# Two mixture-of-experts layers around a state-space block: the first layer's expert outputs stored in slot order and fetched by place

## What is computed

```python
x = L0_attn_x                                                  # (4, 512, 128)
x = _layernorm(x + _L0_attn_ref(x, L0_attn_W_qkv, L0_attn_W_out), axis=-1)
x = _layernorm(x + _L0_ffn_ref(x, ...), axis=-1)
x = _layernorm(x + _L1_attn_ref(x, ...), axis=-1)
x = _layernorm(x + _L1_ffn_ref(x, ...), axis=-1)
```

## Time and profile before

| what | us |
|---|---|
| median of 3 runs (lowest, highest) | 663.41 (660.64, 665.27) |
| the profiled execution's own time | 663.71 |
| its span, first to last instruction | 661.9 |
| first layer: routing and shared MLP | about 74 to 96 |
| first layer: slots | about 96 to 199 |
| fetches to the start of the state loop | about 199 to 235 |
| state loop, four sequences | about 235 to 476 |
| second mixture: routing, slots, end | about 476 to 662 |

### The profile page before, as it was taken

How to read it: one execution, slowest core, us unless ns; L and a number is a source line. 1 busy time by engine, 2 the same in 40 slices (tenths; PEclk the granted TensorE clock), 3 DMA queues, 4 the chain that set the end, 5 groups by cost and what they waited for, 6 DMA issues and landing times.

```text
span 661.9 us, 8700 instructions
## 1 busy us (share of the span) xinstructions
PE 554.6 (84%) x2858; PEld 370.4 (56%) x2858; DVE 419.7 (63%) x756; ACT 361.4 (55%) x640; POOL 383.4 (58%) x303
## 2 busy tenths in 40 slices
PE   6988889999997569679967986988788699999980
PEld 3666556777665224225323532433347699999950
DVE  2444581111106899999999999999967544444456
ACT  3544564555452657944795597768423255555423
POOL 1011117777771246995797689678821677677451
PEclk9999998999999879869988998898989699999986
DMA  4154101111117844343344334433200111111142
GB/s 111 47 179 149 44 7 50 48 47 52 47 39 246 332 172 155 131 158 128 132 139 165 128 127 144 162 123 132 81 16 1 40 42 48 43 43 45 28 130 63
DMA packets 35148, 65.78 MB, mean 99 GB/s; under 512 B 6112, under 2 KB 23208, under 8 KB 34465
## 3 DMA queue, kind: packets, MB, share of 16 engines
q1 hardware_dynamic: 29824, 51.19, 23.2%
q0 software_dynamic: 4992, 9.32, 5.5%
q10 hardware_dynamic: 288, 4.72, 2.0%
HBM read 57.60 MB, written 8.52 MB: 100 GB/s over the span
## 4 chain that ended last, share of the span: by engine, by line
PE 36%; DVE 34%; issue 10%; POOL 9%; ACT 6%; DMA 3%; SPq 0%; POOLq 0%; DVEq 0%; ACTq 0%
DVE wide L1631 11%; DVE ps L1624 6%; PE ps L646 5%; PE ps L650 5%; DVE w L1631 5%; PE ps L658 5%; PE ps L673 4%; PE ps L797 3%; PE ps L686 3%; ACT work L1168 2%; PE ps L679 2%; POOL rows L1807 2%; DVE work L1496 2%; POOL y_choice L1815 1%; DVE work L1407 1%
## 5 line engine op out<-in xcount | busy, mean ns | idle before, releaser
L1807 POOL DMA_INDIRECT rows<-xn_rows,source x78 | 76.2, 977 | 59.0 <-DVE dest L1422 22.1
L1631 DVE TENSOR_TENSOR_SCAN wide<-work,ps 128x1024 f32<-128x1024 f32 x43 | 98.2, 2284 | 1.3
L797 PE MATMUL ps<-wide,ident 128*128 128x512 f32 x128 | 72.1, 691 | 24.6 <-POOL wide L1779 24.6
L1624 DVE TENSOR_TENSOR ps<-ps,w 128x1024 f32<-128x1024 f32 x64 | 78.9, 1233 | 6.9 <-DVE wide L1631 0.5
L1446 DVE COPY xT<-ps 128x128 f32<-128x128 f32 x78 | 22.5, 288 | 83.1 <-PE ps L668 81.5
L797 PE MATMUL ps<-w,ident 128*128 128x512 f32 x124 | 63.5, 641 | 10.5 <-POOL w L1779 10.5
L1779 POOL TENSOR_TENSOR wide<-wide,w 128x1024 f32<-128x1024 f32 x22 | 51.9, 2358 | 32.4 <-DVE wide L1631 32.3
L1168 ACT ACTIVATE work<-work,a_neg 128x512 f32<-128x512 f32 x86 | 56.7, 711 | 19.7 <-DVE wide L1631 17.2
L1451 DVE TENSOR_TENSOR wide<-wide,ps 128x512 f32<-128x512 f32 x39 | 26.8, 688 | 62.5 <-PE ps L650 61.3
L797 PEld LDWEIGHTS ps<-wide,ident 128*128 128x128 f32 x128 | 24.9, 208 | 61.3 <-POOL wide L1779 38.2
L1779 POOL TENSOR_TENSOR w<-wide,w 128x1024 f32<-128x1024 f32 (+1 forms) x21 | 49.0, 2337 | 12.5 <-DVE wide L1631 12.4
(11 more groups left out here) (273 smaller groups left out, 1174.1 us busy)
## 6 DMA issues: line engine op xcount, KB each, us to landing
w<-bc_rows SPq DMA_DIRECT2D x64, 512.0 KB, 3.7
w<-in_w ACTq DMA_DIRECT2D x2, 2304.0 KB, 9.8
w<-y_choice SPq DMA_DIRECT2D x16, 256.0 KB, 3.8
wg<-in_wg SPq DMA_DIRECT2D x1, 2304.0 KB, 11.2
wu<-in_wu SPq DMA_DIRECT2D x1, 2304.0 KB, 16.1
wd<-in_wd SPq DMA_DIRECT2D x1, 2304.0 KB, 21.1
rows<-xn_rows,source POOLq DMA_INDIRECT x78, 2.6
work<-in_x SPq DMA_DIRECT2D x4, 256.0 KB, 2.8
```

What stands on the lines that cost most here:

```text
L797: last = mm_(bank(6 + h), ident[:, :], hc[j % 4][:, h, :], start=False, stop=(j == NS - 1))
L1624: V.tensor_tensor(dbu, du, bc_all[j % 4][:, 0:S].unsqueeze(1).to_broadcast([P, EH, S]), ALU.mult)\
L1631: V.tensor_tensor_scan(st[n % 3].rearrange("p h t -> p (h t)"), dA[n % 3].rearrange("p h t -> p (h t)"), dbu.rearrange("p h t -> p (h t)") ...
L1807: G.indirect_dma_start(out=xin[i % RING][:, :], out_offset=None, in_=xn_rows, in_offset=bass.IndirectOffsetOnAxis(ap=source[:, i:i + 1], a ...
```

## The change

In the first layer only:
- SP stores each slot's output as it stands to `y_slots`, one row per place in the sorted order. The scatters are gone; `dest` is not computed. `posf`, cast to an integer (`place`), says where each token's two rows lie. After the last store has landed GpSimd fetches them: 16 tiles times 2 choices, 32 indirect DMAs (`fetch`).
- VectorE copies each slot's 512 up columns to `own_g`, two slots ahead (`up_weights`). Four products with the copy as the stationary matrix replace the one of 512 columns, the four transposes of the hidden values and the copy to `hT`. The output product of slot i stands in step i, no longer one step later.
- ScalarE issues the loads of `wg`, `wu` and `wd` at steps 4, 13 and 22 of the slot loop.
- Groups 2 and 3 are combined and normalised inside the state loop's first sequence: `combine` and `variances` between product and scan of states 1 and 4, `norm_group` at states 3 and 6. Their choices lie in `nT_all` and their base in `x_all`. Group 0 is combined tile by tile as its fetches land.
- TensorE's last shared products wait for the third tile's fetches in place of SP's.

```diff
@@ -196,8 +197,16 @@
-        all_stats, all_mv = (wide[:, T + at:T + at + NT * n] for at, n in ((0, 6), (96, 2)))
-        all_stats = all_stats.rearrange("p (t s) -> p t s", s=6); all_mv = all_mv.rearrange("p (t s) -> p t s", s=2)
+        all_stats = sb("all_stats", [P, NT, 6]); all_mv = sb("all_mv", [P, NT, 2])
...
+        def base_tile(l, t):
...
+            return x_tile(t) if l == 0 and t >= 2 * QT else tile_of(base[l], t)
...
+        def y_tile(l, c, t):
...
+            return tile_of(nT_all, c * 2 * QT + t - 2 * QT) if l == 0 and t >= 2 * QT else tile_of(y_k[c], t)
@@ -319,6 +331,7 @@
+        LOAD_AT = {4: (wg, "wg"), 13: (wu, "wu"), 22: (wd, "wd")}
@@ -398,19 +411,23 @@
+                if l == 0:
+                    for i in range(ROUTED):
+                        sp.wait_ge(*yout_set[0].at(i + 1))
+                        sp.dma_start(y_slots[i * P:(i + 1) * P, :], yout[i % RING][:, :]).then_inc(slot_sent[i % RING], 16)
+                    return
...
-            load_weights(ld_f1, (wg, "wg"), (wu, "wu"), (wd, "wd"))
@@ -660,32 +677,28 @@
-                    x, h, t, y = i + 2, i + 1, i, i - 1
+                    x, h, y = i + 2, i + 1, i
...
-                        e = expert_of(h)
-                        pe.wait_ge(*xT_set[l].at(h + 1))
-                        last = mm_(bank(hbank[0] + p), xT[p][:, :], wa[:, ds(e, HID)], start=True, stop=True)
-                    if valid(t):
-                        p = i % 2
-                        pe.wait_ge(*hs_set[l].at(t + 1))
+                        pe.wait_ge(*xT_set[0].at(h + 1))
+                        pe.wait_ge(weights_in, h + 1)
...
-                            last = tr(ps[:, 2 + p, j * P:(j + 1) * P], hs[p][:, j * P:(j + 1) * P], ident[:, :])
-                        last.then_inc(hT_ps[l].sem, 1)
+                            last = mm_(ps[:, hbank[0] + p, j * P:(j + 1) * P], own_g[p][:, j * P:(j + 1) * P], xT[p][:, :],
+                                       start=True, stop=True)
...
-                        pe.wait_ge(*hT_set[l].at(y + 1))
+                        pe.wait_ge(*hs_set[0].at(y + 1))
...
-                            last = mm_(bank(y_bank[l][p], D), hT[p][:, j * P:(j + 1) * P], wc[:, ds(e + j * D, D)],
+                            last = mm_(bank(y_bank[0][p], D), hs[p][:, j * P:(j + 1) * P], wc[:, ds(e + j * D, D)],
@@ -701,10 +714,9 @@
-            pe.wait_ge(*hT_set[0].at(ROUTED))
...
-            pe.wait_ge(*gathered[0][0].at(32))
+            pe.wait_ge(first_fetched[2], 32)
@@ -1024,21 +1036,20 @@
-                    h, t, y = i + 1, i, i - 1
+                    h, y = i + 1, i
...
-                    if valid(t):
-                        p = i % 2
-                        act.wait_ge(*hT_ps[l].at(t + 1))
-                        cp(hT[p], bank(2 + p)).then_inc(hT_set[l].sem, 1)
...
-                        wait_pos(act, ys_sent[l][q], y // RING * 16)
-                        cp(yout[q][:, :], bank(y_bank[l][y % 2], D)).then_inc(yout_set[l].sem, 1)
+                        if y >= RING:
+                            act.wait_ge(slot_sent[q], y // RING * 16)
+                        cp(yout[q][:, :], bank(y_bank[0][y % 2], D)).then_inc(yout_set[0].sem, 1)
+                    if i in LOAD_AT:
+                        dst, name = LOAD_AT[i]
+                        act.dma_start(dst[:], a[name]).then_inc(ld_f1, 16)
@@ -1418,6 +1429,9 @@
+                    if l == 0:
+                        V.tensor_copy(place[:, :], posf[:, :, :].rearrange("p k t -> p (k t)")).then_inc(idx_set[0].sem, 1)
+                        return
@@ -1437,6 +1451,10 @@
+                def up_weights(i):
+                    e = expert_at(mybir.EngineType.DVE, 0, i)
+                    V.tensor_copy(own_g[i % 2], w1[:, ds(e, HID)]).then_inc(weights_in, 1)
@@ -1451,9 +1469,15 @@
+                    if l == 0 and valid(i + 3) and i >= -1:
+                        dve.wait_ge(*h_ps[0].at(i + 2))
+                        up_weights(i + 3)
...
+                    dve.wait_ge(*expert_set[0].at(1))
+                    up_weights(0)
+                    up_weights(1)
@@ -1482,18 +1506,31 @@
-                V.tensor_tensor(tiles(base[l][:, b * S:(b + 1) * S]), x_seq(b), tiles(bank(sy_bank(l, b))),
+                V.tensor_tensor(x_seq(b) if l == 0 and b >= 2 else tiles(base[l][:, b * S:(b + 1) * S]), x_seq(b), tiles(bank(sy_bank(l, b))),
...
-                own = [tile_of(base[l], b * QT + q) for q in range(QT)]
-                dve.wait_ge(*gathered[l][b % 2].at((b // 2 + 1) * 32))
+                own = [base_tile(l, b * QT + q) for q in range(QT)]
+                if l:
+                    dve.wait_ge(gathered[b % 2], (b // 2 + 1) * 32)
...
+                if l == 0 and b == 0:
+                    for q in range(QT):
+                        dve.wait_ge(first_fetched[q], 32)
+                        link(V.scalar_tensor_tensor(out=own[q], in0=tile_of(y_k[0], q), scalar=gates[0][:, q:q + 1],
+                                                    in1=own[q], op0=ALU.mult, op1=ALU.add))
+                        link(V.scalar_tensor_tensor(out=own[q], in0=tile_of(y_k[1], q), scalar=gates[1][:, q:q + 1],
+                                                    in1=own[q], op0=ALU.mult, op1=ALU.add))
+                        link(V.bn_stats(all_stats[:, q, :], own[q]))
+                        steps.mark(V.bn_aggr(all_mv[:, q, :], all_stats[:, q, :]))
+                    return
+                if l == 0:
+                    dve.wait_ge(y_fetched[b - 1], QT * 32)
...
-                        steps.mark(V.scalar_tensor_tensor(out=own[q], in0=tile_of(y_k[k], t), scalar=gates[k][:, t:t + 1],
+                        steps.mark(V.scalar_tensor_tensor(out=own[q], in0=y_tile(l, k, t), scalar=gates[k][:, t:t + 1],
@@ -1637,6 +1674,12 @@
+                        if b == 0 and j in (1, 4):
+                            g = 2 + j // 4
+                            combine(0, g)
+                            variances(0, g)
+                        if b == 0 and j in (3, 6):
+                            norm_group(1 + j // 3)
@@ -1658,14 +1701,8 @@
-            combine(0, 2)
-            variances(0, 2)
...
-            combine(0, 3)
-            variances(0, 3)
-            norm_group(2)
...
-            norm_group(3)
@@ -1780,6 +1817,8 @@
+                    if b == 0 and j in (1, 4):
+                        inverse_group(0, 2 + j // 4)
@@ -1787,8 +1826,23 @@
-                for g in range(NB):
-                    inverse_group(0, g)
...
+                def fetch(t):
+                    for c in range(2):
+                        G.indirect_dma_start(out=y_tile(0, c, t), out_offset=None, in_=y_slots,
+                                             in_offset=bass.IndirectOffsetOnAxis(ap=place[:, c * NT + t:c * NT + t + 1], axis=0))\
+                            .then_inc(first_fetched[t] if t < QT else y_fetched[t // QT - 1], 16)
...
+                pool.wait_ge(*idx_set[0].at(2))
+                for k in range(RING):
+                    pool.wait_ge(slot_sent[k], 16 * fetches(k))
+                for t in range(QT + 1):
+                    fetch(t)
+                inverse_group(0, 0)
+                for t in range(QT + 1, NT):
+                    fetch(t)
+                    if t == 2 * QT + 2:
+                        inverse_group(0, 1)
@@ -1807,7 +1861,7 @@
-                    if i >= RING:
+                    if l and i >= RING:
```

More of the change, by code:

```diff
@@ L100, in build @@
         y_choice = nc.dram_tensor("y_choice", (2 * T, D), F32).ap()
+        y_slots = nc.dram_tensor("y_slots", (ROUTED * P, D), F32).ap()
         bc_rows = nc.dram_tensor("bc_rows", (NB * NS, 2 * S), F32).ap()
@@ L163, in build @@
         held_i = sb("held_i", [P, ROUTED], U32); source = sb("source", [P, ROUTED], U32)
-        dest = sb("dest", [P, ROUTED], U32)
+        dest = sb("dest", [P, ROUTED], U32); place = sb("place", [P, PAIRS], U32)
         slot_e = sb("slot_e", [P, ROUTED], I32)
@@ L289, in build @@
         yout_set = layers("yout_set", ROUTED)
-        ys_sent_ = [layers(f"ys_sent{k}", 16 * fetches(k)) for k in range(RING)]
+        ys_sent_ = [layers(f"ys_sent{k}", 0) for k in range(RING)]
+        slot_sent = [sem(f"slot_sent{k}") for k in range(RING)]
         ys_sent = [[r[l] for r in ys_sent_] for l in range(2)]
-        gathered_ = [layers(f"gathered{k}", NB // 2 * 32) for k in range(2)]
-        gathered = [[r[l] for r in gathered_] for l in range(2)]
+        gathered = [sem(f"gathered{k}") for k in range(2)]
+        first_fetched = [sem(f"first_fetched{q}") for q in range(QT)]
+        y_fetched = [sem(f"y_fetched{b}") for b in range(1, NB)]
+        weights_in = sem("weights_in")
         fix_mid = sem("fix_mid")
@@ L1527, in norm_group @@
                 for t in range(g * QT, g * QT + QT):
-                    last = V.tensor_scalar(x_tile(t), tile_of(base[0], t), all_mv[:, t, 0:1], inv2[:, 0, t:t + 1],
```

(1 more changed line is left out.)

18 lines of the change are left out of this document (9 added, 9 removed).

## The result

The changed kernel takes 668.28 us (median of 8 runs, 666.52 to 671.17), the kernel before 663.88 us (8 runs, 660.64 to 665.27). The ratio is 1.0065, with a 95% interval from 1.0047 to 1.0083: 4.4 us slower, within the 1% that was named, and inside the range. The forecast was 664.2.

What follows compares the result with a forecast made beforehand. GpSimd's gathers and scatters bound the slot loop, VectorE the state loop. Terms -18.9 + 4.1 - 0.3 + 10.6 + 5.3 = +0.8 us on the profiled execution gave 664.2 us, range 655 to 672.

Steps and rivals of the forecast that it cites:

- The slot loop: First layer's 39 slots: 1.90 us a slot on TensorE, loop 77.1 us against 96.0, a gain of 18.9 us.
- 2.7 us of ramp: Slot loop: extra time beyond 39 periods, taken from the second layer's loop and added to the new loop.
- The hand-over: From last output copy to first variances: store, fetches and statistics take 15.1 us against 11.0, a loss of 4.1 us.
- From the variances to the state loop: Chain before the first state product: one norm 1.0 us late, another norm leaves its place; net -0.3 us.
- The state loop: Inserted combinations and norms lengthen states 1 to 6 by 10.6 us, waiting for GpSimd's weighing adds 5.3 us.
- the sum itself: All terms added, +0.8 us on the profiled execution of 663.7 us; forecast median 664.2 us, chance 0.42.
- A: Rival: no waiting between VectorE and GpSimd in the states; -5.3, 658.9 us; chance 0.20.
- B: Rival: the work inserted in the states is free, the boundary between sequences waits for something else; 648.3 us; chance 0.08.
- C: Rival: TensorE's clock falls after idling and stays at 1.2 GHz through the convolution; +7.1, 671.3 us; chance 0.10.
- D: Rival: gathers in the slot loop stall behind weight loads; 669.2 us; chance 0.10.
- E: Rival: slot takes 2.10 us for 1.90, +7.8, 672.0 us; chance 0.10. In "E + 3.9": end of last output copy.

Runs made afterwards that it cites:

- e4: The kernel before with only the new slot form on TensorE, ScalarE and VectorE, scatters and read-back kept; 663.23 us, ratio 0.9955.
- e11: The kernel before with three of the eight gather semaphores split by layer, 19 different semaphores on indirect transfers; 667.64 us against 663.82.
- e2: The kernel before with seven of the eight gather semaphores split by layer, 23 different semaphores on indirect transfers; 667.59 us, ratio 1.0037.
- e1: The changed kernel with its 32 fetches signalling on seven of the second layer's scatter semaphores instead of seven of their own; 664.68 us, ratio 0.9989.
- e10: The changed kernel with fetches on 16 semaphores, inserts moved to states 0, 2 and 4, GpSimd's weighings of states 1 and 3 held back; 659.02 us, ratio 0.9935.
- e12: The changed kernel with the three weight loads issued by SP behind its row stores instead of by ScalarE inside the slot loop; 674.66 us.
- e5: The changed kernel with the four scalings ahead of the two small products in the normalisations of groups 2 and 3; 693.74 us against 702.4.
- e8: The kernel before with all eight gather and six of eight scatter semaphores split by layer, 30 different semaphores; 703.66 us against 702.4.
- e9: The changed kernel itself, run again beside the kernel before on another chip; 669.32 us, ratio 1.0068.

## Why the prediction was right, and where it was not

The time lay in the range and on the side named, but 4.1 us above the forecast, and nearly all of that is a thing that was in no term. The terms that were in the sum came out at -2.5, +1.8, -0.5 and +0.1 us against their forecasts and partly cancel, which is luck.

1. **The slot loop**, -18.9: it was -21.4. The period of 1.90 was right. The "2.7 us of ramp" from the second layer did not come: 175.22 - 100.64 is 74.6 us, 39 periods of 1.90 and 0.5 more. The ramp of the second layer held a stretch at 1.2 GHz (eight products in 1.92 us at 519.42, 1.06 later; the granted clock from 518 to 522 us was 0.50). In the first layer TensorE ran its first slots at 1.2 GHz before (102 to 104 us), but at 2.4 after:

```profile
102.00:104.00 2.00, 2.00 (x5) 0.85 (x5) 0.29 (x1) 0.68 (x2) 1.39 (x3) 0.50 0.29 33
```

```profile
102.00:104.00 2.00, 2.00 (x20) 2.00 (x19) 1.27 (x4) 1.07 (x3) 1.55 (x2) 1.00 0.33 57
```

The first row is before, the second after, with the columns of the earlier trace rows: the third figure from the end, 0.50 and 1.00, is the granted clock. The new form alone did not bring it, as e4 shows.

2. **The hand-over**, +4.1: it was +5.9. Of the 1.8 us missing, 1.4 lie in the 2.5 us for the store and two hand-shakes: the first fetch came at E + 3.9 (the stores' bytes moved until 178.0, which is E + 2.8, and GpSimd started 1.1 us later). Some 0.6 more lie in the last tile's sums and statistics, 1.6 us for 1.0 (190.59 to 192.15). The 1.28 between fetches was 1.25, which gives 0.2 back.

3. **From the variances to the state loop**, -0.3: it was -0.8 (25.9 us for 26.7).

4. **The state loop.** Sum 15.9 predicted, 16.0 measured, but by two errors that cancel: the inserted work is 9.67 us and not 10.6, the waiting for GpSimd 6.35 and not 5.3. The value named for the first combination to lose entirely was 2.4 (it lost 2.64); I took the middle between its being lost and not, and it was lost. The others: 1.02 for 1.1, and 1.35 and 1.30 for 1.5 each.

Together -0.3 us at state 7, where +0.8 was forecast. From here on the two executions differ by more than the change. From state 7 to the last product of the loop the kernel before took 214.9 us, and e11 and e2, with the same instructions there, 211.2 and 215.8; the changed kernel took 214.0, so its lead of 1.2 us at the last product says nothing of the change. Behind the loop the clock fell to 1.2 GHz at 478 us in the changed kernel's execution and not in the other's (both had 0.50 from 492 to 496). After, then before:

```profile
478.00:480.00 2.00, 2.00 (x3) 0.71 (x3) 1.86 (x5) 0.00 (x0) 1.10 (x1) 0.50 0.00 0
```

```profile
478.00:480.00 2.00, 1.61 (x4) 0.87 (x5) 1.93 (x4) 0.00 (x0) 1.78 (x2) 1.00 0.00 0
```

Four products of 512 columns took 3.32 us there instead of 1.98. That is the execution's luck more than the change's. The same four products took 3.31 us in e4 and 3.09 in e11, which have the old fetches, and 1.98 in e1 and e10, which have the new ones. And the profiled execution of e1 gained 4.7 us on the changed kernel's between the end of the state loop (474 us) and the second layer's counting (500 us), and came to 658.9 us, where its median is 664.7.

5. **The step that failed** is the sum itself: it took the time to be the last instruction's plus a constant. What it starts from, "the profiled execution, 663.7 us (its span is 661.9)", ended on two things at once, the landing of the last rows at 661.6 and GpSimd's drain at 661.6, and only the first was looked at. The drain rose by 4.1 us and had no cover. With it the sum comes out: 0.5 + 4.0 = 4.5 us of span. The medians say the same without the single executions: where the drain is short (e1), the changed kernel stands at 0.9989 (0.9964 to 1.0013) of the kernel before, so all other terms together are -0.7 us, with 1.6 either way.

The rivals: A (no waiting) fell with the rows above. B (inserts free) fell; all 16 us lengthened the states. C (the clock) happened and was absorbed as argued: TensorE stood idle 6.8 us, the 16 products at 188.09 took 3.37 us at 1.2 GHz, the clock was back in 192 to 194, and the convolution took its 7.14 us. D: gathers did land later, 4.7 us instead of 2.6 by the median of 104 to 215 us, but no slot waited. The Trainium skill's rule that a DMA engine takes turns between its queues (DMA: Bandwidth & Descriptors, section SWDGE vs HWDGE vs iDMA) agrees with this and with e12, where no fetch took over 8.8 us to land beside loads of 9.2, 15.2 and 20.0 us: slower, not behind a whole load. E: the period held.

## What to carry to other kernels

Read what ends last on every engine, the end-of-program instructions too: a path that ends level with the one you shorten or lengthen is the next bound, and here a handful of semaphores was worth as much as the whole change. VectorE sums, products and scalings that have all their operands in SBUF waited out a GpSimd weighing of 128x1024 beside them, however small they were; where GpSimd has slack, hold GpSimd back rather than VectorE. And a part that removes a bound (taking away the scatters) and a part that can only then show (the slot form) have to be costed together, as do loads and the transfers that will run beside them.

## What the runs showed that was not expected

- GpSimd's closing drain: 5.3 to 5.9 us with 16 different semaphores on indirect transfers, 9.2 to 10.0 with 19 to 30. It does not follow the number of transfers (156 in the kernel before with 5.88 us and in e2 with 9.22; 149 in e1 with 5.30 and in the changed kernel with 9.96).
- Scalings with one tensor operand wait for GpSimd like sums of two: 2.34 us for 1.11 (e5).
- Chips differ, and not by one factor. On the chip of e5 to e8 the slots of the kernel before (as e8) end at 217.28 us instead of 196.66 (20.6 us later, not the 18 of e9's expectation), those of the changed kernel (as e5) at 184.40 instead of 175.22; e5, which is the changed kernel but for the order of two normalisations, took 693.74 us in its one run, against 702.4 for the kernel before (699.87 to 705.88). The change would probably pay there. What is slower on that chip was not found, and the changed kernel itself was not run on it.
